# The first batch's rows, adjacency and first weight are loaded and used ahead of the other weights

## The chip, the cores and the metric

The kernel runs on one core of one Trainium2 chip. The metric is the device time of the whole program in microseconds (us). Engines: TensorE (PE, with its weight loads PEld), VectorE (DVE), ScalarE (ACT), GpSimd (POOL), and SyncE (SP), which here issues every DMA on one queue.

## What is computed

32 graphs ("batches") of 512 nodes with 256 features each pass four pre-norm layers, each added to its input. Layer 0 aggregates over neighbours and runs a two-matrix perceptron with an RMS norm between; layer 1 is a sigmoid attention over edges; layer 2 is an 8-head softmax attention biased by the adjacency; layer 3 is a graph convolution. The change concerns the beginning of layer 0 of the first batch.

```python
def layer0(x, adjacency, epsilon, W1, b1, rms_weight, W2, b2):
    neighbor_sum = jnp.einsum('bnm,bmd->bnd', adjacency, x)
    agg = epsilon * x + neighbor_sum
    h = jnp.einsum('bnd,dh->bnh', agg, W1) + b1      # D = 256 -> H = 1024
    h = jax.nn.silu(_rmsnorm(h, rms_weight))
    out = jnp.einsum('bnh,hd->bnd', h, W2) + b2
    return out

h = jnp.maximum(_layernorm(x, axis=-1), 0.0)
x = x + layer0(h, adj, ...)
...
h = jnp.maximum(_layernorm(x, axis=-1), 0.0)
x = x + layer1(h, adj, nodemask, ...)      # W, b, a1, a2, att_b
# layers 2 and 3 likewise, on every batch
```

## The kernel before

Every engine has its own program, written out by hand in program order, and they meet at semaphores. The work on one batch is cut in two halves: the front half (layers 0 and 1) and the back half (layers 2 and 3). `phases(t, tf, nx)` interleaves the back half of batch t, the front half of batch tf and the start (layer norm and aggregate) of batch nx. The program is `phases(None, 0, 1)`, `phases(0, 1, 2)`, a loop of 29 passes of `phases(t, t + 1, t + 2)`, and two closing calls. Before them stands a setup, and the start of batch 0 by itself.

The setup. SP issues all weight loads first (W1 and W2 of 1 MB each, four attention matrices, W3, WL and WLn of 256 KB each, the biases, the 512 KB broadcast of `rmsw`, and the small `cst`), all on the semaphore `w_loaded`, and behind them x, adjT, mask and adj of batch 0. ACT, DVE and PE wait until all of `w_loaded` is there. ACT rounds each weight to a "hi" part (`hi`, L486), DVE takes the remainder as a "lo" part (`lo`, L680), so that a product is made of three passes (`product`, L1026 to L1028). DVE also prepares the bias rows `b1_rows` (L690, L680), `rmsw_b` (L694), small constants in `drv` (L697 to L703), eight blocks of `neg_mask` (L706), and takes `wa` and `s_const` (L716 to L718) from products that PE makes of WLn and `cst` (L1038, L1041). DVE counts its steps in `setup_dve`; at 36 PE, ACT and POOL go on.

The start of batch 0. DVE: `stats0` (L727 to L738), then `diagonal` (L752, L754), which adds epsilon to the adjacency's diagonal. POOL: four small operations of the layer norm (L372 to L381), then `add_b2` (L389). ACT: `norm0` (L500), four Relu. PE: `aggregate` (L1056), eight fp32 matmuls that the trace shows as 16. ACT and DVE split the result in `T_hi` (L486) and `T_lo` (L680).

The hidden layer. Per tile n of 128 rows: PE `hidden` (L1068, L1026 to L1028) in two halves c, ACT `square` (L529), POOL the RMS (L398 to L402), DVE `hid` (L773), ACT tanh (L536), DVE silu (L779), PE `turn_hidden` (L1079), ACT `s_hi` (L486), DVE `s_lo` (L680), and PE `down` with W2 in four quarters of six 128x256 matmuls. The steps of a tile stand at fixed places of a grid, `tile_steps(g)`: tile n is at its step u = g + 4 - 8n, so tile 1 follows tile 0 by eight grid places. In `phases(None, 0, 1)` nothing else stands in the grid.

The changed kernel's lines below the setup are numbered a few higher or lower than before; the words on rows name the lines of the kernel before.

## Time and profile before

| | us |
|---|---|
| median of 3 runs (3794.12 to 3798.18) | 3794.47 |
| the profiled execution's own time | 3793.83 |
| its span in the trace | 3792.0 |
| PE busy | 3595.9 (95%) |
| DVE busy | 2623.7 (69%) |
| ACT busy | 2279.2 (60%) |
| POOL busy | 772.2 (20%) |

The span is the time from the first to the last recorded instruction; the execution's own time is 1.83 us longer. The busy shares are averages over the whole span and say little about a stretch of 70 us at its start; for that stretch one reads the timeline, where each row is an instruction or a run of like ones with what ended the idle time before it. The first matmul of a batch starts at 40.90 us.

### The profile page before, as it was taken

What the parts mean: (1) busy time and instruction counts of PE and PEld (TensorE: products, weight loads), DVE (VectorE), ACT (ScalarE), POOL (GpSimd) and SP (SyncE); (2) the same over time, 40 slices, a digit from 0 to 9 for tenths busy, and PEclk for the clock granted to TensorE, in tenths of its full rate; (3) what the DMA queues carried; (4) which work ended last, traced back from release to release, by engine and by line L of the source; (5) the groups of instructions that cost most, each with busy time, mean ns of one, the idle gap of its engine ahead of it and who ended that gap; (6) DMA issues with size and microseconds to landing.
All of it is one profiled execution on the core that took longest, in us unless ns stands there. A gap on an engine that the chain in (4) does not pass through costs nothing.

```text
span 3792.0 us, 67268 instructions
## 1 busy us (share of the span) xinstructions
PE 3595.9 (95%) x19375; PEld 2445.7 (64%) x19596; DVE 2623.7 (69%) x6436; ACT 2279.2 (60%) x5029; POOL 772.2 (20%) x1611
## 2 busy tenths in 40 slices
...
GB/s 85 62 85 72 56 89 56 89 74 69 67 78 67 89 67 67 78 57 87 85 71 56 89 56 89 75 70 67 78 67 89 67 67 78 57 87 85 65 45 67
DMA packets 166936, 275.09 MB, mean 73 GB/s; under 512 B 23906, under 2 KB 59874, under 8 KB 166756
## 3 DMA queue, kind: packets, MB, share of 16 engines
...
## 4 chain that ended last, share of the span: by engine, by line
PE 61%; issue 13%; DVE 12%; POOL 8%; ACT 5%; POOLq 0%; DMA 0%; DVEq 0%; SPq 0%; another core or an unknown queue 0%; ACTq 0%
PE turn L1213 9%; PE front L1026 7%; PE score L1203 6%; PE front L1027 6%; PE front L1028 6%; PE score L1204 4%; PE value L1228 3%; POOL small L374 3%; PE front L1056 3%; PE front L1079 3%; PE score L1177 3%; PE value L1189 3%; DVE pT L813 2%; ACT hf L500 2%; PE front L1068 2%
## 5 line engine op out<-in xcount | busy, mean ns | idle before, releaser
L588 ACT ACTIVATE prob<-prob,small 128x512 f32<-128x512 f32 x1024 | 736.1, 719 | 375.4 <-DVE small L888 373.8
L888 DVE CUSTOM_DVE_ANT_0 prob<-score,adj_sb,drv 128x512 f32<-128x512 f32 x1024 | 759.4, 747 | 224.8 <-PE score L1204 126.9
L1213 PE MATMUL turn<-ident,prob 128*128 128x128 f32 x4096 | 617.1, 276 | 14.6 <-ACT pT L597 8.7
L1213 PEld LDWEIGHTS turn<-ident,prob 128*128 128x128 f32 x4096 | 484.9, 141 | 134.8 <-issue 62.0
L597 ACT ACTIVATE pT<-turn 128x512 f32<-128x512 f32 x768 | 446.5, 584 | 144.6 <-PE turn L1213 144.6
L1203 PE MATMUL score<-qk_stack 128*128 128x512 f32 x1024 | 496.0, 488 | 31.5 <-DVE small L888 29.9
L1026 PE MATMUL front<-w_hi,s_hi 128*128 128x256 f32 x1024 | 353.0, 345 | 28.6 <-DVE x_in L792 28.6
L1204 PE MATMUL score<-unlinked,neg_mask 128*128 128x512 bf16 x803 | 313.6, 391 | 0.0
L680 DVE TENSOR_TENSOR s_lo<-front,s_hi 128x512 fp32r<-128x512 f32 x320 | 217.7, 680 | 102.7 <-ACT s_hi L486 102.6
L1027 PE MATMUL front<-w_lo,s_hi 128*128 128x256 f32 x1024 | 288.0, 281 | 0.0
L1028 PE MATMUL front<-w_hi,s_lo 128*128 128x256 f32 x1024 | 287.6, 281 | 0.0
L1026 PEld LDWEIGHTS front<-w_hi,s_hi 128*128 128x128 f32 x1024 | 196.0, 191 | 114.2 <-issue 52.6
L1228 PE MATMUL value<-pT,vals 128*32 128x512 f32 x2048 | 252.9, 600 | 5.1 <-issue 5.1
L421 POOL TENSOR_TENSOR inv_x<-small,drv 128x128 f32<-128x128 f32 x256 | 94.7, 401 | 784.0 <-DVE small L904 784.0
L1056 PE MATMUL front<-adjT_f,hid 128*128 128x512 f32 x512 | 232.0, 596 | 20.2 <-ACT hid L500 18.0
L486 ACT ACTIVATE s_hi<-front 128x512 fp32r<-128x512 f32 x320 | 187.5, 586 | 98.4 <-PE front L1111 94.5
L398 POOL TENSOR_TENSOR small<-small 128x1 f32<-128x1 f32 x128 | 24.7, 193 | 1083.3 <-ACT aside L529 1083.3
L773 DVE SCALAR_TENSOR_TENSOR hid<-front,small,rmsw_b 128x512 f32<-128x512 f32 x256 | 180.1, 745 | 88.8 <-POOL small L402 88.8
L1254 PE MATMUL score<-prob,hb 128*128 128x512 f32 x512 | 234.3, 601 | 4.5 <-ACT hb L500 4.5
L1203 PEld LDWEIGHTS score<-qk_stack 128*128 128x128 f32 x1024 | 195.0, 190 | 60.2 <-DVE small L888 54.5
L1111 PE MATMUL front<-pT,hf 128*128 128x512 f32 x512 | 227.5, 597 | 1.6 <-DVE pT L813 1.6
L897 DVE COPY pT<-turn 128x512 f32<-128x512 f32 x256 | 175.9, 687 | 75.8 <-PE turn L1213 73.9
...
## 6 DMA issues: line engine op xcount, KB each, us to landing
qk_stack<-qk SPq DMA_DIRECT2D x1024, 128.0 KB, 2.4
adjT_f<-in_adjT SPq DMA_DIRECT2D x32, 1024.0 KB, 5.0
adj_sb<-in_adj SPq DMA_DIRECT2D x32, 1024.0 KB, 7.9
prob<-in_adjT SPq DMA_DIRECT2D x32, 1024.0 KB, 5.4
x_new<-in_x SPq DMA_DIRECT2D x32, 512.0 KB, 3.7
out<-x_out SPq DMA_DIRECT2D x32, 512.0 KB, 3.1
pT<-in_W SPq DMA_DIRECT2D x2, 1024.0 KB
rmsw_b<-in_rmsw SPq DMA_DIRECT2D x1, 512.0 KB
```

Of the source, the lines that this page charges most:

```text
L588: act.activation(prob[:, i % 8, :], prob[:, i % 8, :], ACT.Exp, bias=nmax[:, h, n:n + 1], scale=-1.0, accum_out=prsum[:, h, n:n + 1]).then ...
L597: act.activation(pT[:, h % HG, j, :], TB[k % 2][:, :], ACT.Copy).then_inc(pT_act, 1)
L888: dve.tensor_tensor_reduce(out=prob[:, i % 8, :], in0=SB_[i % 2][:, :], in1=adj_sb[:, n, :], scale=neg_w[:, h:h + 1], scalar=3e38, op0=ALU ...
L1026: pe.matmul(ps, a[0], b[0], start=start, stop=False)
L1027: pe.matmul(ps, a[0], b[1], start=False, stop=False)
L1028: return pe.matmul(ps, a[1], b[0], start=False, stop=stop)
L1056: last = pe.matmul(FB[d][:, :], h0[:, m, tile(d)], adjT_f[:, m, :], start=(m == 0), stop=(m == NT - 1))
L1203: pe.matmul(SB_[i % 2][:, :], qk_stack[:, h % 4, 0, tile(n)], qk_stack[:, h % 4, 1, :], start=True, stop=False)
L1204: pe.matmul(SB_[i % 2][:, :], neg_mask[:, h, :], unlinked[:, n, :], start=False, stop=True).then_inc(sc_ps, 1)
L1213: last = pe.transpose(TB[k % 2][:, tile(n)], prob[:, (4 * h + n) % 8, tile(j)], ident[:, :])
L1228: last = pe.matmul(VB[HD * h:HD * h + HD, :], vals[:, j, P * g + HD * h:P * g + HD * h + HD], pT[:, h, j, :], start=(j == 0), stop=(j == N ...
L1254: last = pe.matmul(SB_[d][:, :], hb[:, m, tile(d)], adjT_b[:, m, :], start=(m == 0), stop=(m == NT - 1))
```

## The change

On SP the order of the loads becomes: x of batch 0, `cst` (own semaphore `cols_loaded`), adjT of batch 0, then W1, b1 and `rmsw` (own semaphore `w1_loaded`), then W2, W3, WL, WLn, the biases and the four attention matrices (`w_loaded`), then mask and adj. The same transfers are issued, no other ones. On DVE `stats0` and `diagonal` stand first; then `prepare_w1` (five steps: the bias rows, `rmsw_b`, `w1_lo`); the rest, `prepare_rest` (26 steps), stands inside the grid of `phases(None, 0, 1)`, behind the steps of grid place 3. On ACT `norm0` comes first, `w1_hi` behind it, and the other three rounded weights behind `aggregated(0, 1)`. On PE the two aggregates come first, the products with WLn and `cst` (`shared_products`) behind `hidden` of tile 0, and the wait for all 36 steps of DVE stands at grid place 6. On POOL `add_b2` waits for `w_loaded`.

```diff
+        cols_loaded, w1_loaded = sem("cols_loaded"), sem("w1_loaded")
...
-            sp.dma_start(region[:, 0:2048].rearrange("p (k n) -> p k n", k=DT), W1.rearrange(kp, p=P)).then_inc(w_loaded, 16)
-            sp.dma_start(region[:, 2048:4096].rearrange("p (k n) -> p k n", k=FT), W2.rearrange(kp, p=P)).then_inc(w_loaded, 16)
-            for i, w in enumerate((WqT, WkT, WvT, WoT)):
-                sp.dma_start(ws[:, i, :, :], w.rearrange(kp, p=P)).then_inc(w_loaded, 16)
-            sp.dma_start(w3_stage, W3.rearrange(kp, p=P)).then_inc(w_loaded, 16)
-            sp.dma_start(wl_stage, WL.rearrange(kp, p=P)).then_inc(w_loaded, 16)
-            sp.dma_start(region[:, 7168:7680].rearrange("p (k n) -> p k n", k=DT), WLn.rearrange(kp, p=P)).then_inc(w_loaded, 16)
-            for r in (0, 32):
-                sp.dma_start(region[r:r + 1, 4096:4096 + F], b1[None, :]).then_inc(w_loaded, 16)
-            sp.dma_start(rmsw_b[:, :], rmsw[None, :].to_broadcast([P, F])).then_inc(w_loaded, 16)
-            for d, s in ((bL_b, bL), (b2_b, b2), (b3_b, b3)):
-                sp.dma_start(d[:, :], s[None, :].to_broadcast([P, D])).then_inc(w_loaded, 16)
-            sp.dma_start(cst[:, :], cols).then_inc(w_loaded, 16)
...
+            sp.dma_start(cst[:, :], cols).then_inc(cols_loaded, 16)
             load_adjT_f(0)
+            sp.dma_start(region[:, 0:2048].rearrange("p (k n) -> p k n", k=DT), W1.rearrange(kp, p=P)).then_inc(w1_loaded, 16)
+            for r in (0, 32):
+                sp.dma_start(region[r:r + 1, 4096:4096 + F], b1[None, :]).then_inc(w1_loaded, 16)
+            sp.dma_start(rmsw_b[:, :], rmsw[None, :].to_broadcast([P, F])).then_inc(w1_loaded, 16)
+            sp.dma_start(region[:, 2048:4096].rearrange("p (k n) -> p k n", k=FT), W2.rearrange(kp, p=P)).then_inc(w_loaded, 16)
+            sp.dma_start(w3_stage, W3.rearrange(kp, p=P)).then_inc(w_loaded, 16)
+            sp.dma_start(wl_stage, WL.rearrange(kp, p=P)).then_inc(w_loaded, 16)
+            sp.dma_start(region[:, 7168:7680].rearrange("p (k n) -> p k n", k=DT), WLn.rearrange(kp, p=P)).then_inc(w_loaded, 16)
+            for d, s in ((b2_b, b2), (bL_b, bL), (b3_b, b3)):
+                sp.dma_start(d[:, :], s[None, :].to_broadcast([P, D])).then_inc(w_loaded, 16)
+            for i, w in enumerate((WqT, WkT, WvT, WoT)):
+                sp.dma_start(ws[:, i, :, :], w.rearrange(kp, p=P)).then_inc(w_loaded, 16)
...
-            pool.wait_ge(setup_dve, SETUP_DVE)
...
             layernorm(0, 0, f_norm, norm_tiles(0))
+            pool.wait_ge(w_loaded, N_W)
             add_b2(0)
+            pool.wait_ge(setup_dve, 5)
...
-            act.wait_ge(w_loaded, N_W)
...
-            hi(w1_hi[:, :, :], region[:, 0:2048].rearrange("p (k n) -> p k n", k=DT)).then_inc(setup_act, 1)
-            hi(w2_hi[:, :, :], region[:, 2048:4096].rearrange("p (k n) -> p k n", k=FT)).then_inc(setup_act, 1)
-            hi(wl_hi[:, :, :], wl_stage).then_inc(setup_act, 1)
-            hi(w3_hi[:, :, :], w3_stage).then_inc(setup_act, 1)
-            act.wait_ge(setup_dve, SETUP_DVE)
...
             norm0(0)
+            act.wait_ge(w1_loaded, N_W1)
+            hi(w1_hi[:, :, :], region[:, 0:2048].rearrange("p (k n) -> p k n", k=DT)).then_inc(setup_act, 1)
             aggregated(0, 0)
             aggregated(0, 1)
+            act.wait_ge(w_loaded, N_W)
+            hi(w2_hi[:, :, :], region[:, 2048:4096].rearrange("p (k n) -> p k n", k=FT)).then_inc(setup_act, 1)
+            hi(wl_hi[:, :, :], wl_stage).then_inc(setup_act, 1)
+            hi(w3_hi[:, :, :], w3_stage).then_inc(setup_act, 1)
...
+            def prepare_w1():
+
+                dve.wait_ge(w1_loaded, N_W1)
+                b1_stage = region[:, 4096:4096 + F]
+                for r in (0, 32):
+                    done(dve.tensor_copy(b1_rows[r:r + 1, :], b1_stage[r:r + 1, :]))
+                done(lo(b1_rows[32:33, :], b1_stage[32:33, :], b1_rows[32:33, :]))
+                done(dve.tensor_scalar(rmsw_b[:, :], rmsw_b[:, :], 0.5 * float(F) ** 0.5, None, ALU.mult))
+                dve.wait_ge(setup_act, 1)
+                done(lo(w1_lo[:, :, :], region[:, 0:2048].rearrange("p (k n) -> p k n", k=DT), w1_hi[:, :, :]))
+                assert step[0] == SETUP_W1, step[0]
...
+            def prepare_rest():
+
+                dve.wait_ge(setup_act, 4)
+                done(lo(w2_lo[:, :, :], region[:, 2048:4096].rearrange("p (k n) -> p k n", k=FT), w2_hi[:, :, :]))
+                done(lo(wl_lo[:, :, :], wl_stage, wl_hi[:, :, :]))
+                done(lo(w3_lo[:, :, :], w3_stage, w3_hi[:, :, :]))
+                for w, sgn, mag in ((cst[:, 8:16], t8, t8b), (cst[:, 6:8], t2, t2b)):
+                    done(dve.tensor_scalar(sgn, w, 0.0, 2.0, ALU.is_ge, ALU.mult))
...
+                for h in range(H):
+                    done(dve.tensor_scalar(neg_mask[:, h, :], ident[:, :], t8[:, h:h + 1], -BIG, ALU.mult, ALU.mult))
+                dve.wait_ge(setup_pe, 1)
+                for c in range(2):
+                    done(dve.tensor_copy(wa[:, c, :], SB_[c][:, 0:D]))
+                done(dve.tensor_copy(t2, VB[:, 0:2]))
+                done(dve.tensor_scalar(s_const, t2[:, 0:1], t2[:, 1:2], cst[:, 17:18], ALU.add, ALU.add))
...
+                    if prepare is not None and g == 3:
+                        prepare()
...
             stats0(0)
+            dve.wait_ge(cols_loaded, 16)
+            dve.wait_ge(setup_pool, 7)
             diagonal(0)
+            prepare_w1()
             aggregated(0, 0)
             aggregated(0, 1)
             restore_diagonal(0)
-            phases(None, 0, 1)
+            phases(None, 0, 1, prepare_rest)
             phases(0, 1, 2)
...
+            def shared_products():
+
+                pe.wait_ge(w_loaded, N_W)
+                wln = region[:, 7168:7680].rearrange("p (k n) -> p k n", k=DT)
+                for c in range(2):
+                    for k in range(DT):
+                        pe.matmul(SB_[c][:, 0:D], cst[:, 2 * k + c:2 * k + c + 1].to_broadcast([P, P]), wln[:, k, :],
...
+                if shared is not None:
+                    shared()
                 for g in GRID:
+                    if shared is not None and g == 6:
+                        pe.wait_ge(setup_dve, SETUP_DVE)
                     if b and 0 <= g < 4 * H - 4:
...
+            pe.wait_ge(setup_dve, 5)
             aggregate(0, 0)
             aggregate(0, 1)
-            phases(None, 0, 1)
+            pe.wait_ge(setup_dve, SETUP_W1)
+            phases(None, 0, 1, shared_products)
```

Three places of the programs, as they stand in order. First ACT from its start. The names: `w_hi` and `wl_hi` are the rounded weights, `hid<-x_new` is `norm0`, `T_hi` is the rounded aggregate, `aside` with `squared` and `hid_ps` is `square`. Before:

```order
L486 ACT_TABLE_LOAD
L486 ACTIVATE w_hi<-pT 128x2048 [waits w_loaded]
L486 ACTIVATE w_hi<-pT 128x2048
L486 ACTIVATE wl_hi<-pT 128x512
L486 ACTIVATE w_hi<-pT 128x512
L500 ACTIVATE hid<-x_new,small 128x256 [waits front_normed,setup_dve]
L500 ACTIVATE hid<-x_new,small 128x256 x3
L486 ACTIVATE T_hi<-front 128x512 [waits agg_ps] x2
L529 ACTIVATE aside,small<-front 128x512 [waits diag_back,hid_ps]
L529 ACTIVATE aside,small<-front 128x512 [waits squared,hid_ps]
```

and now:

```order
L492 ACT_TABLE_LOAD
L492 ACTIVATE hid<-x_new,small 128x256 [waits front_normed]
L492 ACTIVATE hid<-x_new,small 128x256 x3
L485 ACTIVATE w_hi<-pT 128x2048 [waits w1_loaded]
L485 ACTIVATE T_hi<-front 128x512 [waits agg_ps] x2
L485 ACTIVATE w_hi<-pT 128x2048 [waits w_loaded]
L485 ACTIVATE wl_hi<-pT 128x512
L485 ACTIVATE w_hi<-pT 128x512
L521 ACTIVATE aside,small<-front 128x512 [waits diag_back,hid_ps]
L521 ACTIVATE aside,small<-front 128x512 [waits squared,hid_ps]
```

The four Relu moved ahead of every weight; one weight stands ahead of `T_hi`, and three stand between `T_hi` and the first `square`, behind a wait for `w_loaded`.

Second DVE in the grid of `phases(None, 0, 1)`, from `hid` of tile 0 on. Before, tile 1's `hid` follows tile 0's `s_lo` directly:

```order
L773 SCALAR_TENSOR_TENSOR hid<-front,small,rmsw_b 128x512 x2
L779 SCALAR_TENSOR_TENSOR hid<-aside,hid 128x512 x2
L680 TENSOR_TENSOR s_lo<-front,s_hi 128x512 x2
L773 SCALAR_TENSOR_TENSOR hid<-front,small,rmsw_b 128x512 x2
L779 SCALAR_TENSOR_TENSOR hid<-aside,hid 128x512 x2
L680 TENSOR_TENSOR s_lo<-front,s_hi 128x512
```

Now, from the same `hid` of tile 0:

```order
L772 SCALAR_TENSOR_TENSOR hid<-front,small,rmsw_b 128x512 x2
L778 SCALAR_TENSOR_TENSOR hid<-aside,hid 128x512 x2
L678 TENSOR_TENSOR s_lo<-front,s_hi 128x512 x2
L678 TENSOR_TENSOR w_lo<-pT,w_hi 128x2048
L678 TENSOR_TENSOR wl_lo<-pT,wl_hi 128x512
L678 TENSOR_TENSOR w_lo<-pT,w_hi 128x512
L704 TENSOR_SCALAR drv<-cst 128x8
L705 TENSOR_SCALAR drv<-drv 128x8
L706 TENSOR_TENSOR drv<-cst,drv 128x8
L707 TENSOR_SCALAR drv<-drv 128x8
L704 TENSOR_SCALAR drv<-cst 128x2
L705 TENSOR_SCALAR drv<-drv 128x2
```

Behind tile 0's `s_lo` the preparation of W2, WL and W3 and all the small constants came in; of the 26 steps the first nine are shown, and behind the last of them stands tile 1's `hid`.

Third PE at the end of tile 1's `hidden`, ahead of tile 0's `down` (`front<-w_hi,s_hi`). Before:

```order
L1026 MATMUL front<-w_hi,T_hi 128x512
L1027 MATMUL front<-w_lo,T_hi 128x512
L1028 MATMUL front<-w_hi,T_lo 128x512
L1026 MATMUL front<-w_hi,s_hi 128x256 [waits s_lo_ready,s_hi_ready]
L1027 MATMUL front<-w_lo,s_hi 128x256
L1028 MATMUL front<-w_hi,s_lo 128x256
L1026 MATMUL front<-w_hi,s_hi 128x256
```

and now:

```order
L1030 MATMUL front<-w_hi,T_hi 128x512
L1031 MATMUL front<-w_lo,T_hi 128x512
L1032 MATMUL front<-w_hi,T_lo 128x512
L1030 MATMUL front<-w_hi,s_hi 128x256 [waits s_lo_ready,s_hi_ready,setup_dve]
L1031 MATMUL front<-w_lo,s_hi 128x256
L1032 MATMUL front<-w_hi,s_lo 128x256
L1030 MATMUL front<-w_hi,s_hi 128x256
```

The matmuls are the same; the first one of `down` also waits for `setup_dve`.

## Rows read from the trace of the kernel before

**Rows 1.** The page: busy time, share of the span and instructions.

```profile
PE 3595.9 (95%) x19375; PEld 2445.7 (64%) x19596; DVE 2623.7 (69%) x6436; ACT 2279.2 (60%) x5029; POOL 772.2 (20%) x1611
```

**Rows 2.** DMA view, 10.5 to 41 us: KB, then us from issue to landing.

```profile
adjT_f<-in_adjT SPq DMA_DIRECT2D x1, 1024.0 KB, 11.2
adj_sb<-in_adj SPq DMA_DIRECT2D x1, 1024.0 KB, 12.0
x_new<-in_x SPq DMA_DIRECT2D x1, 512.0 KB, 9.0
```

**Rows 3.** DMA view, 41 to 60 us: the second batch's x alone.

```profile
x_new<-in_x SPq DMA_DIRECT2D x1, 512.0 KB, 3.4
```

**Rows 4.** Timeline, 0 to 14 us, SP's DMA issues: start, length, issue.

```profile
0.75 0.44 SPq L246 DMA_DIRECT2D pT<-in_W  x1
...
10.92 0.43 SPq L263 DMA_DIRECT2D x_new<-in_x  x1
11.40 0.56 SPq L272 DMA_DIRECT2D adjT_f<-in_adjT  x1
...
13.30 0.88 SPq L269 DMA_DIRECT2D adj_sb<-in_adj  x1
```

**Rows 5.** Timeline, 18 to 34 us: the weights' preparation on ACT, PE and DVE.

```profile
18.47 3.71 ACT L486 ACTIVATE w_hi<-pT 128x2048 fp32r<-128x2048 f32 x2 [16.44 <-DMA cst<-in_cols]
...
18.50 3.78 PE L1038 MATMUL front<-pT,cst 128*128 128x256 f32 x8 [18.50 <-DMA cst<-in_cols]
18.55 1.40 DVE L690 CAST b_rows<-pT 1x1024 fp32r<-1x1024 f32 x2 [15.72 <-DMA cst<-in_cols]
...
21.96 0.17 DVE L697 TENSOR_SCALAR drv<-cst 128x8 f32<-128x8 f32 x1
...
22.61 0.62 ACT L486 ACTIVATE w_hi<-pT 128x512 fp32r<-128x512 f32 x1
...
28.21 4.62 DVE L680 TENSOR_TENSOR w_lo<-pT,w_hi 128x2048 fp32r<-128x2048 f32 x2
32.86 0.88 DVE L716 COPY wa<-front 128x256 f32<-128x256 f32 x2
```

**Rows 6.** Timeline, 34 to 52 us: start of batch 0.

```profile
34.28 1.40 DVE L727 BATCH_NORM_STATS2 small<-x_new 128x6 f32<-128x256 f32 x4
...
38.58 2.77 POOL L389 TENSOR_TENSOR x_in<-x_new,b_b 128x256 f32<-128x256 f32 x4
...
40.90 9.03 PE L1056 MATMUL front<-adjT_f,hid 128*128 128x512 f32 x16 [17.98 <-ACT hid L500]
...
50.59 0.69 DVE L680 TENSOR_TENSOR T_lo<-front,T_hi 128x512 fp32r<-128x512 f32 x1 [2.74 <-ACT T_hi L486]
```

**Rows 7.** Timeline, 53 to 62 us: tile 0 of the hidden layer.

```profile
53.98 0.60 ACT L529 ACTIVATE aside<-front 128x512 f32<-128x512 f32 x1 [0.95 <-PE front L1028]
...
55.88 1.41 DVE L773 SCALAR_TENSOR_TENSOR hid<-front,small,rmsw_b 128x512 f32<-128x512 f32 x2 [4.26 <-POOL small L402]
...
58.07 0.82 PE L1079 MATMUL front<-ident,hid 128*128 128x128 f32 x4 [4.13 <-DVE hid L779]
...
61.30 0.69 DVE L680 TENSOR_TENSOR s_lo<-front,s_hi 128x512 fp32r<-128x512 f32 x1 [1.05 <-ACT s_hi L486]
```

**Rows 8.** Timeline of DVE: tile 1's `hid`, with its wait.

```profile
68.04 1.41 DVE L773 SCALAR_TENSOR_TENSOR hid<-front,small,rmsw_b 128x512 f32<-128x512 f32 x2 [6.04 <-POOL small L402]
```

**Rows 9.** Windows: us, busy PE, PEld, DVE, ACT, POOL, then granted clock, DMA, GB/s.

```profile
42.00:44.00 2.00, 2.00 (x4) 0.90 (x3) 0.00 (x0) 0.00 (x0) 0.00 (x0) 1.00 0.61 205
...
58.00:60.00 2.00, 1.30 (x6) 0.91 (x7) 1.15 (x3) 1.23 (x2) 0.00 (x0) 0.61 0.00 0
...
64.00:66.00 2.00, 2.00 (x8) 1.57 (x7) 0.00 (x0) 0.44 (x2) 0.00 (x0) 0.69 0.00 0
66.00:68.00 2.00, 2.00 (x19) 2.00 (x17) 0.00 (x0) 0.69 (x2) 0.94 (x3) 1.00 0.00 0
```

**Rows 10.** Waits, 200 to 3700 us: total, times, longest.

```profile
DVE qk L874 <- issue: 56.6, 28, 2.3
```

More of the change, by code:

```diff
@@ L199, in gnn_kernel @@
         assert len(freed) == N_turned and N_turned % 2 == 0
-        SETUP_DVE = 36
+        SETUP_W1, SETUP_DVE = 10, 36
         def tile_steps(g):
@@ L340, in _ @@
             sp.wait_ge(out_stored, 16 * B)
-        N_W = 16 * 16
+        N_W1, N_W = 16 * 4, 16 * 11
         @block.gpsimd
```

53 lines of the change are left out of this document (13 added, 40 removed).

## The prediction

> **What bounds the kernel now.** The page says that PE is busy 95% of the span [rows 1]; that is the 31 later stretches, in which PE is the limit and which the change leaves as they are. The first batch is another matter: there one chain of small steps ends last, and the timeline of the first 70 us has to be read row by row. Three waits should be seen. First, ACT, PE and DVE all stand still until 18.5 us for the last weight transfer, and DVE then prepares weights until 34.28 [rows 5, 6]. Second, x landed at 10.92 + 9.0 = 19.9 us and adjT at 11.40 + 11.2 = 22.6 [rows 2, 4], long before DVE gets to them. Third, only then comes the layer norm, and PE's first aggregate starts at 40.90, having been idle for 17.98 us [rows 6]. From there on the chain is aggregate, `T_lo`, `square`, `hid`, silu, turn, `s_lo` [rows 6, 7], and DVE stands idle for 6.04 us between tile 0 and tile 1 [rows 8]. What one gains is the time by which this chain moves forward, less what the moved work puts back into it; nothing behind it is tied to an absolute time, since all loads of batch 0 are there by 13.30 + 12.0 = 25.3 us [rows 2, 4].
>
> **Step A, the early start.** x is now SP's first issue, at 0.75 us [rows 4]. Alone on the queue a load of x takes 3.4 us from issue to landing [rows 3], which gives 4.15, the lower bound. For the upper bound I go back from the old queue: x, adjT and adj landed in their order, 19.9, 22.6 and 25.3, so 1024 KB take 2.7 us; what stood ahead of x was some 4750 KB (W1, W2 and the four attention matrices 3072, three of 256, `rmsw` 512, three of 128, small ones 17), 12.5 us, and 19.9 - 12.5 = 7.4. x is now alone ahead of everything, as in the row of the load alone, but it is the first issue after the launch, so I take 4.7, near the lower end. From the first statistics (34.28) to the first aggregate (40.90) it is 6.62 us [rows 6]: aggregate at 11.3 us, 29.6 earlier. adjT, 1033 KB behind x, lands about 2.7 us later at 7.4 to 10.1; `diagonal`, 1.2 us, is done before 11.3 either way and costs nothing; its cover is the norm on POOL and ACT.
>
> **Step B, W1 in time?** T_lo's second half ended at 50.59 + 0.69 = 51.28, 10.38 behind the aggregate's start [rows 6], so it would end at 21.7. What must be ready by then: W1, b1 and `rmsw` are 1544 KB behind adjT, so they land 4.1 us after it; counted back from 22.6, when everything up to the attention matrices is there (the same set of bytes that was there when adjT landed before), 3200 KB or 8.4 us, it is 14.2 at the latest. DVE then needs 21.96 - 18.55 = 3.4 us for the bias rows and `rmsw_b`, and 4.62 / 2 = 2.3 for `w1_lo` [rows 5]: 19.9. The first T_lo (0.7) ends at 20.6, before the second can start at 21.0. ACT's `w1_hi` (3.71 / 2 = 1.9) ends at 16.1 and T_hi of the first half is due at about 17. Cost: nothing; the cover is the aggregate of 9.03 us [rows 6], with 0.4 us to spare at the worst.
>
> **Step C, three weights ahead of `square`.** ACT now waits for `w_loaded`, 22.6 us, then rounds W2, WL and W3. Before, all four took 18.47 to 23.23, so without W1's 1.86 it is 2.9 us [rows 5]: ACT is free at 25.5. `square` was ready to start about 1.06 us behind T_lo, now 22.8. So the two squares run from 25.6, back to back, 0.7 each, to 27.0, where they ended at 53.98 + 0.69 = 54.67 [rows 7]. The shift falls from 29.6 to 27.7. The start of the squares now hangs on `w_loaded` and no longer on x: even with x at 7.4 they would be ready at 25.5. POOL's `add_b2` (2.77 us [rows 6]) waits for the same transfer and ends at 25.4, ahead of the RMS: nothing. PE's `shared_products` start behind `hidden` of tile 0, near 24.4, and take 3.78 us and four tiny matmuls more [rows 5], say 5 at most, to 29.4; PE's next work, the turn, came 58.07 - 54.67 = 3.4 behind the squares [rows 7], now 30.4. Nothing either; they lie in what was an idle gap of 4.13 us.
>
> **Step D, the DVE block of 26 steps.** Tile 0's last `s_lo` ended at 61.99 [rows 7], now 61.99 - 27.7 = 34.3. The block: from 21.96 to 32.86 all of it ran but for one `w_lo` too many, 10.90 - 2.31 = 8.59, and from 32.86 to 34.28 the last four, 1.42 [rows 5, 6]: 10.0 us. It ends at 44.3. The gap that covers it was 6.05 us (61.99 to 68.04 [rows 7, 8]), so 4.0 us stick out: tile 1's `hid` starts at 44.35 against 68.04. Shift now 23.7. ACT's and POOL's work for tile 1 ends in its shadow.
>
> **Step E, PE behind the block.** PE waits for the 36th step at grid place 6, and three of tile 0's four quarters of `down`, 18 matmuls, are queued ahead of tile 1's first turn. Before they ran while PE had nothing else. The turn is due 58.07 - 55.88 = 2.19 us behind `hid` [rows 7], at 46.5. At the full level (2.4 GHz) PE made 17 weight loads in 2 us, 0.118 each [rows 9], 2.1 us: just in time, cost 0. At half (1.2 GHz) 0.235 each, 4.2 us: 2.0 late. Which level? PE has been idle since the end of tile 1's `hidden`, 6 to 9 us. After the idle 4.13 us ahead of 58.07 the granted clock fell to 0.61 and came back only in the slice of 64 to 66 (0.69) [rows 7, 9]; I take half, 2.0 us. If the level holds as long as then, about 7 us of full work, it costs up to 3.5, and 4 with the queueing. Shift: 21.7, between 19.7 and 23.7.
> The rows are not of one voice here: ahead of the aggregate PE was idle for 17.98 us, and still the slice 42 to 44 shows 1.00 [rows 6, 9]; by that row the cost would be nothing. The Trainium skill, "TensorE: Matmul & The Clock Gate", Part 1, says that the throttled state is the default and that activity releases it, and warns that clock events in a trace are not always reliable; by it the `down` matmuls start slow, whatever that one slice shows, the 2.0 us are paid, and the sum is 21.7 instead of 23.7.
>
> **The sum.** 29.6 - 1.9 (C) - 4.0 (D) - 2.0 (E) = 21.7 us. The profiled execution's span 3792.0 becomes 3770.3, its own time 3793.83 - 21.7 = 3772.1; the median lies 0.64 above that execution, so 3772.8 us. Less than 0.2% (7.6 us) either way can't be told from no change.
>
> **Rivals.**
> (1) The weights land later than 22.6, because the order of many small rows costs the queue something. The latest landing of the old queue is adj's, 25.3; every microsecond is paid in full in step C: up to 2.7, time 3773.5 to 3775.5. For it: small broadcasts stand amid the loads. Against: the same bytes in 22.6 before. Chance 0.15.
> (2) PE stays at half through tile 2's `hidden`: 3775 to 3777. Chance 0.12.
> (3) Full level at once, or weights a little earlier: 3770 to 3771. Chance 0.08.
> (4) The change does not do what it says: the transfers share the DMA engines evenly, x lands near 20 as before, and the aggregate starts at 26.5. The shift is 14.4 less C to E, about 8: 3786. Against: three landings in the order of issue, 2.7 us apart [rows 2, 4]. Chance 0.03.
> (5) The other side: the head of the loop. DVE stands 56.6 us in 28 passes, 2.02 each, at the loop's first instruction with nothing that the profile shows to wait for [rows 10]. The waits added to the setup put the loop at another place of the instruction stream. If this gap grew by 0.75 us in each of 29 passes the gain would be gone; from 1.0 us on the kernel would be slower by over 0.2%, and if it doubled, by 58 - 22 = 37 us, 3831. Against: nothing in the body changes, and only a few waits are added ahead of it. Chance 0.06, half of it for small moves of either sign.
>
> **How the numbers follow.** The likeliest (0.56) is 3772.8, own range 3771 to 3775. With rivals (1) to (3) this reaches 3770 to 3777; I put the range at 3768.5 to 3779, which leaves out rival (4), most of (5), and the unusually slow run of three (3798.18, 3.7 above the median). Faster by over 0.2% (below 3786.9): the likeliest with (1) to (3) 0.91, half of (4) and a third of (5), 0.94 in all; within: 0.03; slower: 0.03.
>
> **What would show it.** Right: first aggregate at 10.5 to 13 us; T_lo's second half ending near 21.7; the first `square` waiting on ACT's own roundings until about 25.6, not on PE; tile 1's `hid` behind the block at about 44.3, with no idle DVE ahead; PE's first `down` matmul released by DVE; a period of the loop unchanged at DVE's 2.02 us gap. Wrong: an aggregate after 15 us (A), PE waiting for `w1_lo` at `hidden` (B), `square` released by PE (C), idle DVE ahead of tile 1's `hid` (D), or `down` done before the turn is due (E).

## The result, and the profile after

| | before | after |
|---|---|---|
| time of the runs, median | 3796.32 us (3794.12 to 3800.04, 4 runs) | 3775.03 us (3772.78 to 3777.71, 4 runs) |
| ratio, 95% interval | | 0.9941, 0.9929 to 0.9953 |
| profiled execution, its span | 3793.83, 3792.0 us | 3772.78, 3771.0 us |

The change makes the kernel 0.59% faster, about 21 us, and the interval leaves out 1. The page of after:

```profile
span 3771.0 us, 67491 instructions
...
PE 3599.3 (95%) x19596; PEld 2444.3 (65%) x19596; DVE 2623.8 (70%) x6436; ACT 2278.9 (60%) x5029; POOL 771.7 (20%) x1611
```

PE's busy time is as good as that of [rows 1], 3599.3 us for 3595.9 (the trace of before lacks some records of matmuls, 19375 for 19596). What was gained is idle time. The timeline of the first 30 us (start, length, engine and line; in brackets the idle time ahead and its releaser):

```profile
4.28 1.40 DVE L726 BATCH_NORM_STATS2 small<-x_new 128x6 f32<-128x256 f32 x4 [1.45 <-DMA x_new<-in_x]
...
9.10 0.43 DVE L751 COPY aside<-adjT_f 128x512 f32<-128x512 f32 x1 [3.00 <-DMA adjT_f<-in_adjT]
9.56 0.75 DVE L753 SCALAR_TENSOR_TENSOR adjT_f<-ident,cst,aside 128x512 f32<-128x512 f32 x1
...
10.46 8.79 PE L1060 MATMUL front<-adjT_f,hid 128*128 128x512 f32 x16 [10.46 <-DVE adjT_f L753]
...
16.48 2.29 DVE L678 TENSOR_TENSOR w_lo<-pT,w_hi 128x2048 fp32r<-128x2048 f32 x1
...
19.92 0.69 DVE L678 TENSOR_TENSOR T_lo<-front,T_hi 128x512 fp32r<-128x512 f32 x1 [0.42 <-ACT T_hi L485]
...
23.83 1.91 ACT L485 ACTIVATE w_hi<-pT 128x2048 fp32r<-128x2048 f32 x1 [3.94 <-DMA ws<-in_WoT]
...
23.87 2.77 POOL L388 TENSOR_TENSOR x_in<-x_new,b_b 128x256 f32<-128x256 f32 x4 [15.77 <-DMA ws<-in_WoT]
...
26.68 0.58 ACT L521 ACTIVATE aside<-front 128x512 f32<-128x512 f32 x1
...
29.41 1.41 DVE L772 SCALAR_TENSOR_TENSOR hid<-front,small,rmsw_b 128x512 f32<-128x512 f32 x2 [8.47 <-POOL small L401]
```

Read it against [rows 5, 6]. x was there at 4.28 and adjT at 9.10. The aggregate starts at 10.46, released by DVE's `diagonal` (L753) and not by ACT's norm, which ended at 8.14 + 2.07 = 10.21. T_lo's second half ends at 20.61, 30.7 us earlier than the 51.28 of before. Then comes what is now the late item: ACT stands 3.94 us, PE 0.59 and POOL 15.77 for the same semaphore, w_loaded, which is complete at 23.83 with WoT. The squares start at 26.68 with no idle time ahead, so it is ACT's own three roundings that hold them.

The timeline of after, 35 to 62 us:

```profile
35.44 2.28 DVE L678 TENSOR_TENSOR w_lo<-pT,w_hi 128x2048 fp32r<-128x2048 f32 x1
...
45.11 0.27 DVE L717 TENSOR_SCALAR drv<-drv,cst 128x1 f32<-128x1 f32 x1
45.42 1.41 DVE L772 SCALAR_TENSOR_TENSOR hid<-front,small,rmsw_b 128x512 f32<-128x512 f32 x2
...
45.44 0.58 PE L1030 MATMUL front<-w_hi,s_hi 128*128 128x256 f32 x1 [6.12 <-DVE drv L717]
...
45.82 0.42 PE L1031 MATMUL front<-w_lo,s_hi 128*128 128x256 f32 x1
...
49.44 1.06 PE L1083 MATMUL front<-ident,hid 128*128 128x128 f32 x4
...
57.42 1.41 DVE L772 SCALAR_TENSOR_TENSOR hid<-front,small,rmsw_b 128x512 f32<-128x512 f32 x2 [3.95 <-POOL small L401]
```

The block starts at 35.44, and tile 1's `hid` at 45.42 follows it with no idle time in brackets, where [rows 8] had 6.04 us. PE's `down` is released by the block's last step (L717). How fast PE then runs stands in the windows (us, busy of PE, PEld, DVE, ACT, POOL, then granted clock, DMA share, GB/s):

```profile
44.00:46.00 2.00, 0.56 (x2) 0.57 (x3) 1.86 (x5) 0.00 (x0) 0.00 (x0) 0.64 0.01 4
46.00:48.00 2.00, 2.00 (x12) 2.00 (x11) 1.52 (x3) 0.98 (x2) 0.00 (x0) 0.50 0.00 0
...
50.00:52.00 2.00, 2.00 (x13) 1.90 (x12) 0.83 (x2) 0.60 (x1) 0.00 (x0) 0.65 0.00 0
52.00:54.00 2.00, 2.00 (x11) 1.57 (x10) 1.32 (x3) 0.70 (x2) 0.00 (x0) 1.00 0.00 0
```

The clock is at 0.50 of the full level, which is 1.2 GHz, while the `down` matmuls run, behind 6.12 us in which PE was idle, and is back at 1.00 in the slice from 52. Last, the head of the loop in the view of waits, 200 to 3700 us:

```profile
DVE qk L873 <- issue: 52.1, 26, 2.2
```

26 waits of 2.0 us, against 28 of 2.02 [rows 10]: the loop's head has not moved. Nor has its length: from the issue of batch 2's x to the last issue of that load it is 3339.9 us before and 3340.2 after.

### The profile page after: what moved, and what is told of

It reads as the page before. It is cut to its first block, busy times and chain, and to the rows that moved or that the text cites. A ratio compares the mean times of both kernels' runs of the same rounds, so it can differ in the third digit from the quotient of the medians.

```text
span 3771.0 us, 67491 instructions
## 1 busy us (share of the span) xinstructions
PE 3599.3 (95%) x19596; PEld 2444.3 (65%) x19596; DVE 2623.8 (70%) x6436; ACT 2278.9 (60%) x5029; POOL 771.7 (20%) x1611
## 4 chain that ended last, share of the span: by engine, by line
PE 61%; issue 13%; DVE 12%; POOL 8%; ACT 5%; POOLq 0%; SPq 0%; DMA 0%; DVEq 0%; ACTq 0%
PE turn L1217 9%; PE front L1030 6%; PE score L1207 6%; PE score L1208 6%; PE front L1031 6%; PE front L1032 6%; PE value L1232 3%; POOL small L373 3%; PE front L1083 3%; PE value L1193 3%; PE score L1181 3%; PE front L1060 3%; DVE pT L812 2%; ACT hf L492 2%; POOL x_out L439 2%
## 5 line engine op out<-in xcount | busy, mean ns | idle before, releaser
L1208 PE MATMUL score<-unlinked,neg_mask 128*128 128x512 bf16 x1024 | 398.9, 390 | 0.0
L397 POOL TENSOR_TENSOR small<-small 128x1 f32<-128x1 f32 x128 | 24.7, 193 | 1077.9 <-ACT aside L521 1077.9
L1060 PE MATMUL front<-adjT_f,hid 128*128 128x512 f32 x512 | 231.8, 596 | 12.7 <-DVE adjT_f L753 10.5
```

The costliest lines, as they stand in the source:

```text
L1060: last = pe.matmul(FB[d][:, :], h0[:, m, tile(d)], adjT_f[:, m, :], start=(m == 0), stop=(m == NT - 1))
L1208: pe.matmul(SB_[i % 2][:, :], neg_mask[:, h, :], unlinked[:, n, :], start=False, stop=True).then_inc(sc_ps, 1)
```

## Experiments

Executions of one kernel differ by 2 to 6 us in their time, as much as most of the effects looked for. The traces are steadier. I therefore read a **mark** in each, the start of the issue that loads batch 2's x. A repeat of the unchanged kernel (e11, last run) gave 106.80 against 107.09 for the mark, and `hid` of tiles 0 to 3 within 0.4 us. That is one repeat only, and e4 and e5, which differ from the changed kernel only behind tile 0's `hid`, have it at 29.37 and 29.85 us, up to 0.8 from the repeat's 29.04; so I take no difference under 1 us in these columns for an effect by itself. From the mark to the last issue of that load all kernels took 3339.5 to 3342.1 us. All times are us from the span's start.

| kernel | first aggregate | `hid` tile 0 | tile 1 | tile 2 | tile 3 | mark | span |
|---|---|---|---|---|---|---|---|
| before | 40.90 | 55.88 | 68.04 | 77.82 | 87.61 | 127.64 | 3792.0 |
| after | 10.46 | 29.41 | 45.42 | 57.42 | 67.20 | 107.09 | 3771.0 |
| e1 old load order | 26.36 | 41.28 | 57.33 | 68.50 | 79.27 | 119.41 | 3787.0 |
| e2 ACT's weights late | 11.20 | 28.16 | 44.18 | 56.04 | 66.81 | 107.68 | 3774.8 |
| e3 and POOL's late | 11.12 | 25.98 | 42.42 | 53.49 | 64.24 | 104.31 | 3768.5 |
| e4 block in three | 10.86 | 29.37 | 41.84 | 53.05 | 63.89 | 104.70 | 3772.3 |
| e5 PE kept busy | 11.30 | 29.85 | 45.87 | 55.66 | 66.43 | 106.70 | 3774.5 |
| e6 own semaphore | 10.60 | 26.02 | 42.03 | 53.45 | 64.21 | 104.48 | 3769.0 |
| e7 `cst` behind adjT | 10.56 | 28.73 | 44.77 | 56.15 | 66.93 | 107.16 | 3774.5 |
| e8 e3 with e4 | 11.13 | 26.01 | 38.54 | 48.40 | 59.57 | 100.67 | 3765.4 |
| e9 e8 with e6, e7 | 10.62 | 25.94 | 38.59 | 48.44 | 58.28 | 98.13 | 3764.9 |
| e10 preparation in one | 10.99 | 44.59 | 55.35 | 66.11 | 75.89 | 116.70 | 3784.6 |
| e11 repeat of after | 10.82 | 29.04 | 45.09 | 57.11 | 66.89 | 106.80 | 3773.8 |
| e12 e9, PE kept busy | 10.50 | 25.49 | 37.11 | 46.97 | 56.80 | 96.98 | 3761.1 |

**My theory** was the prediction's sum with one term larger: the first batch starts 30.7 us earlier and gives back 4.1 us at the weights, 3.9 at the block and 2.2 at PE's clock. The rivals: the gain comes from the load order alone (e1, e10), the 4.1 us are ACT's roundings rather than the transfer (e2, e3, e6), and the late turn is queueing rather than clock (e5).

**e1, the old load order.** The weights' issues stand ahead again, `cst`, x and adjT behind them; everything else is the changed kernel.

```diff
-            load_x(0)
-            sp.dma_start(cst[:, :], cols).then_inc(cols_loaded, 16)
-            load_adjT_f(0)
             sp.dma_start(region[:, 0:2048]...W1...).then_inc(w1_loaded, 16)
...
+            sp.dma_start(cst[:, :], cols).then_inc(cols_loaded, 16)
+            load_x(0)
+            load_adjT_f(0)
             load_mask(0)
```

> The changed kernel with the old order of the loads (weights first, then cst, x, adjT of batch 0), all else as changed. If the order of the transfers carries the gain: x lands near 19.9 us as before, the first aggregate starts near 26.1 us instead of 10.46, T_lo's second half ends near 36.3, ACT rounds three weights behind it (2.9 us), tile 0's squares end near 40.6 instead of 28.1, so the time is about 12.5 us over the changed kernel's 3772.8: 3785. If only the programs' order on the engines carries it (the transfers are hidden anyway): 3773.

```profile
22.28 0.43 DVE L751 COPY aside<-adjT_f 128x512 f32<-128x512 f32 x1 [0.90 <-DMA adjT_f<-in_adjT]
...
26.36 8.80 PE L1060 MATMUL front<-adjT_f,hid 128*128 128x512 f32 x16 [26.36 <-ACT hid L492]
...
38.53 0.59 ACT L521 ACTIVATE aside<-front 128x512 f32<-128x512 f32 x1
```

This is before's set of bytes in before's order: adjT is there at 22.28 and the norm's tail releases the aggregate at 26.36. The mark gains 8.2 us on before and lies 12.3 behind after's. So the order of loads is worth 12.3 of the 20.6 us, and the rest is there without it. Here the squares hardly wait for the weights: they end 3.5 us behind T_lo's second half, 3.4 in the kernel before.

**e10, the preparation in one part.** The complement: the new load order, but ACT's roundings, the shared products and all 26 steps come ahead of T_lo, as before.

```diff
             prepare_w1()
+            prepare_rest()
             aggregated(0, 0)
...
-            pe.wait_ge(setup_dve, SETUP_W1)
-            phases(None, 0, 1, shared_products)
+            shared_products()
+            pe.wait_ge(setup_dve, SETUP_DVE)
+            phases(None, 0, 1)
```

> The changed kernel with one part undone: ACT rounds all weights and DVE does all of its preparation in one block ahead of T_lo; only the loads' order and the early norm and aggregate stay. If the two-part preparation is worth what my steps say: T_lo ends near 38.1 instead of 20.6, the squares near 41.5, tile 1's hid near 54.9 with no block ahead of it, marker near 114.6, which is 13 us better than before and 7.5 worse than the change. If the block costs the same wherever it stands: marker at 107.

```profile
26.88 2.29 DVE L678 TENSOR_TENSOR w_lo<-pT,w_hi 128x2048 fp32r<-128x2048 f32 x1 [7.76 <-ACT w_hi L485]
...
41.00 0.60 ACT L521 ACTIVATE aside<-front 128x512 f32<-128x512 f32 x1 [13.26 <-PE front L1033]
```

The aggregate starts at 10.99, but ACT's square then waits 13.26 us for PE, which waited for the block. Mark: 10.9 us ahead of before, 9.6 behind after (9.9 behind its repeat); expected were 13 and 7.5. Loads first and two parts each bring about half; with only one of them the other's wait takes over. Here tile 1 follows tile 0 by 10.76, with no block in between.

**e2, ACT's three roundings later.** They move from ahead of the squares to grid place 3, behind tile 0's `s_hi`; DVE's three `lo` steps go behind the masks, near the block's end.

```diff
-            act.wait_ge(w_loaded, N_W)
-            hi(w2_hi ...); hi(wl_hi ...); hi(w3_hi ...)
-            phases(None, 0, 1)
+            phases(None, 0, 1, round_rest)
...
+                    if rounds is not None and g == 3:
+                        rounds()
```

> ACT rounds W2, WL and W3 at grid place 3, behind tile 0's s_hi, instead of ahead of the squares; DVE's block does its constants first. POOL's add_b2 still waits for w_loaded ahead of the RMS. My theory: the squares are ready to run at about 21.8 and 23.3 and end at 24.0 instead of 28.1, but POOL is still held by add_b2 until 26.6, so the RMS starts at 26.7 instead of 28.27: gain 1.6 us, time 3771.2. Rival (POOL's wait is of no account): gain 4.1, 3768.7. Rival (the roundings ahead of the squares cost nothing): 3772.8.

```profile
22.45 0.60 ACT L521 ACTIVATE aside<-front 128x512 f32<-128x512 f32 x1 [1.78 <-PE front L1036]
...
24.30 2.77 POOL L388 TENSOR_TENSOR x_in<-x_new,b_b 128x256 f32<-128x256 f32 x4 [16.10 <-DMA ws<-in_WoT]
...
27.02 0.19 POOL L397 TENSOR_TENSOR small<-small 128x1 f32<-128x1 f32 x1
```

The squares start at 22.45 and 24.08 instead of 26.68 and 27.44, and 3 us are gained there. But POOL's `add_b2` is queued ahead of the RMS and waits for the same semaphore: from 24.30 to 27.02 it holds L397, which in after began at 28.27. `hid` moves by 1.25 us (the aggregate itself began 0.74 us later, at 11.20, since adjT landed at 9.84), and at the mark nothing is left (0.6 later). The wait had three holders, and one engine freed exposes the next.

**e3, POOL's addition later too.** `add_b2` and its wait now stand behind tile 0's RMS.

```diff
-            pool.wait_ge(w_loaded, N_W)
-            add_b2(0)
             pool.wait_ge(setup_dve, 5)
-            phases(None, 0, 1)
+            phases(None, 0, 1, first_b2)
```

> As the one before, and POOL's add_b2 with its wait for w_loaded stands behind tile 0's RMS. My theory: the squares end at 24.0, hid of tile 0 starts at 25.2 instead of 29.4, nothing takes the place of the wait; gain 4.1 us, profile 3768.7. Rival: PE's shared products, which also wait for w_loaded (23.8) and end at 26.3, come late for the turn (due at 27.4): then less than 4.1.

Tile 0's `hid` comes 3.4 us earlier, the mark 2.8. The aggregate began 0.66 us later here, and from its start to `hid` it is 14.86 us for after's 18.95, 4.1 less, which is the whole of the forecast; median of 4 runs 3774.27 (ratio to before 0.9941, 0.9925 to 0.9958). Its ratio is after's, so the times show no gain, though the mark does. DVE and POOL now meet, in e3's timeline:

```profile
27.43 1.12 DVE L787 SCALAR_TENSOR_TENSOR hid<-aside,hid 128x512 f32<-128x512 f32 x1
...
37.22 2.29 DVE L687 TENSOR_TENSOR w_lo<-pT,w_hi 128x2048 fp32r<-128x2048 f32 x1
37.29 2.27 POOL L397 TENSOR_TENSOR small<-small 128x1 f32<-128x1 f32 x1 [8.17 <-ACT aside L526]
```

L397 adds 128 x 1 elements, 0.19 us elsewhere. Here it takes 2.27 and ends with DVE's `w_lo`, which began 0.07 us earlier. That costs nothing here, since tile 1's `hid` waits for DVE's block and not for POOL. The other direction costs: DVE's silu at 27.43 took 1.12 us instead of 0.69 while POOL's addition ran, and tile 1 follows tile 0 by 16.44 us instead of 16.01.

**e6, the attention matrices on a semaphore of their own.** Nothing is moved on ACT or POOL, but w_loaded no longer counts the four matrices, which only PE's second call needs.

```diff
-                sp.dma_start(ws[:, i, :, :], w...).then_inc(w_loaded, 16)
+                sp.dma_start(ws[:, i, :, :], w...).then_inc(ws_loaded, 16)
...
-        N_W1, N_W = 16 * 4, 16 * 11
+        N_W1, N_W, N_WS = 16 * 4, 16 * 7, 16 * 4
...
+            pe.wait_ge(ws_loaded, N_WS)
             phases(0, 1, 2)
```

> The four attention matrices (1 MB, the last of w_loaded) get a semaphore of their own, for which PE waits ahead of the second phases call. If tile 0's squares hang on w_loaded (term C): it comes some 2.7 us earlier, near 21.1, ACT has rounded at 24.1, the squares run from there, gain 2.6 us, time 3770.2. If not: 3772.8.

```profile
20.44 1.91 ACT L485 ACTIVATE w_hi<-pT 128x2048 fp32r<-128x2048 f32 x1
...
23.28 0.59 ACT L521 ACTIVATE aside<-front 128x512 f32<-128x512 f32 x1
```

ACT does the same roundings at 20.44, 3.39 us earlier, and the squares start at 23.28. `hid` of tile 0 gains 3.4, the mark 2.6. So most of term C (3.4 of 4.1 us) is the wait for a transfer that these engines don't need here, not the roundings: about the gain of e3, by one semaphore.

**e7, `cst` behind adjT.** The 9 KB of `cst` (128 rows of 72 bytes) stood between x and adjT.

```diff
             load_x(0)
-            sp.dma_start(cst[:, :], cols).then_inc(cols_loaded, 16)
             load_adjT_f(0)
+            sp.dma_start(cst[:, :], cols).then_inc(cols_loaded, 16)
```

> The small cst load is issued behind adjT instead of ahead of it. The DMA rate dips to about 50 GB/s at 3.75 us in the changed kernel; if that is cst's small rows, the dip moves behind adjT, adjT lands some 0.8 us earlier (8.2 instead of 9.0) and the first aggregate is released by ACT's Relu at 10.2 instead of DVE's diagonal at 10.46; w_loaded and the time stay (23.8; 3772.8), since the same bytes are ahead of it. If the dip is something at the queue's start: it stays where it is and adjT lands at 9.0.

The moved bytes in slices of 0.375 us, 0 to 15 us, of after, then of e7, and e7's first row on adjT:

```profile
GB/s 0 0 0 0 8 177 289 380 385 199 49 109 224 273 284 311 377 322 393 399 437 410 459 393 415 426 426 437 344 311 268 262 314 287 358 380 385 377 369 366
```

```profile
GB/s 0 0 0 0 11 137 281 390 385 347 126 284 235 360 415 328 333 389 415 407 426 415 415 426 415 426 371 322 232 208 249 314 363 371 380 390 382 361 352 352
```

```profile
7.87 0.43 DVE L751 COPY aside<-adjT_f 128x512 f32<-128x512 f32 x1 [1.81 <-DMA cst<-in_cols]
```

After's rate has a hole of 199, 49 and 109 GB/s at 3.4 to 4.5 us; in e7 only one slice of 126 is left. Both transfers are there at 7.87 instead of 9.10, w_loaded at 23.14 instead of 23.83, and the aggregate is now released by ACT's norm at 10.56, no earlier. Only adjT's landing is clear of scatter: it held DVE until 9.10 to 9.94 us in the nine kernels that have the new order with `cst` ahead of it, and DVE went on at 7.87, 7.93 and 8.21 in the three with `cst` behind. The repeat of after had w_loaded at 23.45 and `hid` at 29.04, so that the 0.7 us gained at each shrinks to 0.3 against it. The mark gains nothing: tile 3 follows tile 2 by 10.78 us instead of 9.78, with the clock at 0.66 and 0.50 from 58 to 62, where after has 1.00.

**e5, PE kept busy.** 22 matmuls of 512 columns, whose output nothing reads, are put ahead of PE's wait for the block. They only keep the engine from standing idle.

```diff
                     if shared is not None and g == 6:
+                        for i in range(22):
+                            pe.matmul(TB[0][:, :], ones_rows[:, :], b1_rows[:, 0:N], start=True, stop=True)
                         pe.wait_ge(setup_dve, SETUP_DVE)
```

> The changed kernel with 22 added matmuls of 128x512 into a PSUM bank that nothing reads yet, on PE ahead of its wait for DVE's 36th step, so that PE is busy for about 5 of the 6.1 us that it idles there. If term E is the clock (PE at half level after the idle time, 18 matmuls of down take 4.2 us instead of 2.1 ahead of tile 1's turn): down's matmuls start 0.12 us apart, the turn starts near 47.6 instead of 49.65, gain 2.0 us, time 3770.8. If the lateness is the queueing alone: the turn stays at 49.6 and the time at 3772.8.

The timeline of e5, and its windows:

```profile
39.40 5.17 PE L1297 MATMUL turn<-b_rows,ones_rows 128*128 128x512 f32 x22
...
45.87 1.41 DVE L772 SCALAR_TENSOR_TENSOR hid<-front,small,rmsw_b 128x512 f32<-128x512 f32 x2
...
45.89 0.39 PE L1030 MATMUL front<-w_hi,s_hi 128*128 128x256 f32 x1 [1.32 <-DVE drv L717]
```

```profile
46.00:48.00 2.00, 2.00 (x17) 2.00 (x18) 1.96 (x3) 0.63 (x1) 0.00 (x0) 1.00 0.00 0
...
56.00:58.00 2.00, 0.14 (x1) 0.14 (x2) 1.77 (x3) 0.73 (x2) 0.00 (x0) 1.00 0.00 0
58.00:60.00 2.00, 2.00 (x12) 2.00 (x12) 1.34 (x2) 1.13 (x2) 0.00 (x0) 0.55 0.00 0
```

The `down` matmuls now follow one another by 0.12 us instead of 0.21 at a granted clock of 1.00, the turn comes 2.25 us behind `hid` as it did before the change (2.19 [rows 7]), and tile 2 follows tile 1 by 9.79 us instead of 12.00. So the 18 queued matmuls fit ahead of the turn at the full clock, and what made them late was the half clock. But the mark gains only 0.4: at 58 the clock is 0.55, behind a stretch in which PE was busy for 0.14 of 2 us, and tile 3 takes 10.77. e7 and four other kernels without a fill have a tile 3 as late, so it isn't shown that the fill brought this on; what is shown is that its gain was not kept.

**e4, the block in three pieces.** W2's `lo` (10 to 11) stays at grid place 3, the constants go to place 11, the masks and sums to place 19; PE waits for step 11 only at place 6, and for all 36 steps ahead of layer 1.

```diff
-                    if prepare is not None and g == 3:
-                        prepare()
+                    if prepare is not None:
+                        prepare(g)
...
+            def prepare_rest(g):
+                if g in (3, 11, 19):
+                    {3: prepare_w2, 11: prepare_consts, 19: prepare_masks}[g]()
...
-                        pe.wait_ge(setup_dve, SETUP_DVE)
+                        pe.wait_ge(setup_dve, SETUP_W2)
```

> DVE's block of 26 steps is cut in three: w2_lo (2.3 us) where the block stood, the other two low parts and the small constants (3.6 us) behind tile 1's s_lo, the masks and wa (4.0 us) behind tile 2's; PE waits only for w2_lo ahead of down. My theory (terms D and E are 4 + 2 us): tile 1's hid starts at 41.3 instead of 45.4, down runs while PE would have waited, the turn is on time; the two later pieces fit in gaps of 4.1 us. Gain 6.1 us, profile 3766.7. Rival (what is cut out comes back in the later gaps): gain 2 or less, 3771 or more.

The windows of e4 around the second and third piece:

```profile
46.00:48.00 2.00, 2.00 (x6) 1.50 (x6) 1.74 (x5) 0.60 (x1) 0.00 (x0) 0.50 0.04 8
...
50.00:52.00 2.00, 2.00 (x15) 1.82 (x14) 1.12 (x7) 0.83 (x4) 0.15 (x1) 1.00 0.00 0
...
56.00:58.00 2.00, 2.00 (x11) 2.00 (x10) 1.97 (x4) 0.62 (x2) 0.00 (x0) 0.50 0.00 0
```

Tile 1's `hid` comes 3.6 us earlier, so D's size is right and the three pieces fit: DVE still idles 1.72 us ahead of tile 2's `hid` and 0.77 ahead of tile 3's. The expected 6.1 us shrank to 2.4 at the mark, because the clock now falls in two other places (0.50 at 46 and at 56) and tiles 2 and 3 follow by 11.21 and 10.84 us. Median of 4 runs 3771.98 (0.9934, 0.9917 to 0.9951), which overlaps with after's interval.

**e8, e3 and e4 together,** and **e9, with e6's semaphore and e7's order as well.**

> The late roundings on ACT, the late add_b2 on POOL and DVE's block in three pieces together. If the terms C (with POOL) and D with E are separate: gain 4.1 + 6.1 = 10.2 us over the changed kernel, profile near 3762.6, 31 us under the kernel before. If they share their cover (ACT's roundings now end later than DVE wants w2_lo): 7 us or less, 3766.

> Everything that helped so far in one kernel: late roundings on ACT, late add_b2 on POOL, DVE's block in three pieces, the attention matrices on a semaphore of their own, cst behind adjT. Prologue marker: the issue of batch 2's x, which stood at 127.64 us before, 107.09 in the changed kernel and 100.67 in the combined one. If the load order's part (adjT landing 1.2 us earlier) and the rest add up: first aggregate near 10.3, marker near 99.8, median about 0.8 under the combined kernel's. If tile 0 is by then held by something else (PE's turn, the half clock): marker at 100.6.

e8's mark is 6.4 us ahead of after's, where the two alone gave 2.8 and 2.4; the miss against 10.2 has several parts: 0.7 us at tile 0, where the aggregate began 0.67 later, 0.5 at tile 1 (the silu took 1.12 us again), 1.4 at tile 3, behind by 11.17 at low clock (0.56 and 0.59 from 52 to 56), and 1.2 more behind it. e9 reaches 98.13, 9.0 ahead of after and 1.7 ahead of what was expected. That is not the doing of the semaphore and of `cst`: tile 2's `hid` comes at 48.44, as in e8 (48.40), and the gain on e8 arises at tile 3, which follows by 9.84 at full clock, and behind it. With the roundings and `add_b2` moved away tile 0's `hid` no longer hangs on w_loaded. Medians of 5 runs each: 3768.55 (0.9922, 0.9908 to 0.9935) and 3767.80 (0.9923, 0.9909 to 0.9936). The two can't be told apart in time; each is some 7 us below after, and the slowest of their ten executions (3769.65) is faster than the fastest of after's five with its repeat (3772.78).

**e12, e9 with PE kept busy:** 8 matmuls without a reader behind the shared products, ahead of the first turn.

```diff
                     shared()
+                    for i in range(8):
+                        pe.matmul(TB[0][:, :], ones_rows[:, :], b1_rows[:, 0:N], start=True, stop=True)
```

> The same as the best version, with 8 added matmuls of 128x512 into an unread PSUM bank behind PE's shared products, which fill the idle time ahead of tile 0's first turn. If the half clock that follows this idle time is what makes tile 1's hid come 12.5 us behind tile 0's (9.8 between later tiles): it comes some 10.7 behind, marker 1.8 us earlier. If ACT's roundings or w2_lo set it: 12.5 as before.

```profile
25.42 3.27 POOL L388 TENSOR_TENSOR x_in<-x_new,b_b 128x256 f32<-128x256 f32 x4
...
33.77 2.29 DVE L687 TENSOR_TENSOR w_lo<-pT,w_hi 128x2048 fp32r<-128x2048 f32 x1 [2.15 <-ACT w_hi L490]
...
35.17 0.94 POOL L397 TENSOR_TENSOR small<-small 128x1 f32<-128x1 f32 x1 [6.48 <-ACT aside L526]
```

All windows from 24 to 60 us show 1.00, where e9 has 0.50 from 30 to 34. Tile 1 follows tile 0 by 11.62 us instead of 12.65. It was to be 10.7, but `w_lo` waits 2.15 us for ACT's rounding, as in e9 (2.14), and POOL's L397, 0.19 us elsewhere, now runs into it: it takes 0.94, and here `hid` waits for POOL. The mark is 1.15 ahead of e9's, of which 0.45 were there at tile 0's `hid`, ahead of any effect of the fill; one execution took 3762.85 us, the shortest of all here, and one execution can't say more.

**e11, the repeat,** gave the scatter named above.

> The changed kernel once more, unchanged, as a measure of how far the marks of one profile move by themselves. If marks are sharper than whole times: batch 2's x is issued within 0.7 us of 107.09, while the span may be 3771 to 3776.

## Why the prediction was right, and where it was off

| shift against before, us | predicted | measured |
|---|---|---|
| first aggregate | 29.6 | 30.4 |
| T_lo's second half, end | 29.6 | 30.7 |
| squares, end (C) | 27.7 | 26.6 |
| tile 1's `hid` (D) | 23.7 | 22.6 |
| tile 2's `hid` (E) | 21.7 | 20.4 |
| span | 21.7 | 21.0 |

**Step A** held: the aggregate at 10.46 for a forecast of 11.3; x landed by 4.28, near the lower bound of 4.15, and POOL's L373 took 1.02 us, where before its like took 1.51. adjT was to land about 2.7 us behind x and took 4.8 (3.6 at most in e7, without `cst` between): the pace of the full old queue was not there in the first microseconds. It still fell into the range of 7.4 to 10.1. One sentence was wrong: `diagonal` "costs nothing". It released the aggregate (10.46 <-DVE), 0.25 us behind the norm, since adjT needed 9.1 us. e7 shows that its cover is that thin.

**Step B** held: `w1_lo` ended at 16.48 + 2.29 = 18.77, ahead of the second T_lo at 19.92. In the repeat the aggregate took 10.16 us instead of 8.79 and T_lo ended at 22.34 instead of 20.61; the squares came no later, at 26.31, since w_loaded held them in both.

**Step C** is the term that was mis-sized: 4.1 us instead of 1.9. What failed is the sentence "now waits for `w_loaded`, 22.6 us": it was 23.83. Rival (1) had named this (later than 22.6, paid in full), and 1.1 us of the miss is that. The other 1.1 us is that T_lo came earlier than forecast, which the squares could not use, as the prediction said of x; so behind step C the sum is off by 1.1 us and not by 2.2. e6 shows the whole price of that wait: 3.4 us at tile 0. Why w_loaded was late stays open: SP's issues ended at 17.8 us instead of 14.2, W3's issue alone taking 4.21, and no run separated that; e7's 23.14 against 23.83 and 23.45 is too little to put it down to `cst`.

**Step D** was right in mechanism and size: 9.94 us of block, 3.9 stuck out (4.0). e4 took 3.6 of them away by undoing it.

**Step E** was right, and so was the choice between the two readings of [rows 6, 9]: 2.2 us measured, 2.0 forecast, and e5 removes all of it by keeping PE busy. The row of 42 to 44 that spoke against it was misleading. The timeline of before has weight loads of 0.34 us inside that very slice, and of 0.19 from 45.04 on:

```profile
42.74 0.34 PEld L1056 LDWEIGHTS front<-adjT_f,hid 128*128 128x128 f32 x1 [0.52 <-issue]
45.04 0.19 PEld L1056 LDWEIGHTS front<-adjT_f,hid 128*128 128x128 f32 x1 [0.26 <-issue]
```

In after too the windows' column shows 1.00 from the aggregate's start, and yet its weight loads tell another clock (after, timeline of PEld):

```profile
12.30 0.33 PEld L1060 LDWEIGHTS front<-adjT_f,hid 128*128 128x128 f32 x1 [0.52 <-issue]
13.16 0.33 PEld L1060 LDWEIGHTS front<-adjT_f,hid 128*128 128x128 f32 x1 [0.52 <-issue]
13.94 0.19 PEld L1060 LDWEIGHTS front<-adjT_f,hid 128*128 128x128 f32 x1 [0.45 <-issue]
14.37 0.19 PEld L1060 LDWEIGHTS front<-adjT_f,hid 128*128 128x128 f32 x1 [0.24 <-issue]
```

They last 0.33 us and follow one another by 0.85 until 13.2, then 0.19 and 0.43: half the pace for the first 3 us (for the first 6 in the repeat). The Trainium skill, "TensorE: Matmul & The Clock Gate", Part 1, warns that clock events in a trace are not always reliable; these rows agree.

**The rivals.** (1) came in part: w_loaded was 1.2 us later than forecast, out of its up to 2.7. (2) is out: full clock from 52 us, tile 3 another 9.78 behind. (3) is out by E. (4) is out: x was there at 4.28. e1 shows what it would have cost, with the aggregate at 26.36 for 26.5 and a shift of 8.2 at the mark for "about 8". But 14.4 less C to E, as written, is 14.4 - 7.9 = 6.5, not 8; in e1 term C cost next to nothing and tile 3 lost 1.0 us at low clock, so the agreement is partly luck. (5) is out by the view of waits and by the length of the loop. The measured profile lies 0.7 us above the forecast and the medians 2.2 (3775.03 for 3772.8), inside the scatter of single executions: after's four spans go from 3771.0 to 3775.9, and the profiled one is the fastest of them. The median is at the edge of the likeliest case's own range, 3771 to 3775, and would suit rival (1) as well. Of the 2.2 us, 1.85 is that before's median moved from 3794.47 to 3796.32 with a fourth run; between the medians it is 21.3 us, and at the mark 20.6, for a forecast of 21.7.

**Left open.** Why the clock falls in some gaps and not in others. Tile 3 follows tile 2 by 9.78 us in after and 10.7 to 10.8 in e1, e2, e3, e5, e6 and e7, with the same instructions. Nor is it known why executions with nearly equal marks differ by 3 us in their span (after, its repeat and e7). Part of it arises in the loop (3340.2, 3342.1 and 3341.4 us from the mark to the last issue of an x) and part behind that issue (323.8, 324.9 and 325.9); at 3690 to 3730 after shows a granted clock of 1.00, e7 0.85 and 0.89.
